# Stacked keys and queries: one contraction of 96 rows for three products of 32, and the values of the same step last in a slot

## The reference

```python
x = x + 0.5 * ffn(layernorm(x))            # weights rounded to -1, 0, 1 times a scale
x = x + attention(layernorm(x))
x = x + 0.5 * ffn(layernorm(x))

# attention: x is 4 x 1024 x 512, 16 heads of 32
kqv = x @ Wqkv + bqkv                      # q, k, v
scores = einsum('bsnh,btnh->bnst', k, q) / sqrt(32)
scores = triu(scores) - 10000 * tril(ones, k=-1)
attn = softmax(scores, axis=2)             # over the last index
out = einsum('bnkq,bknh->bqnh', attn, v)
out = out.reshape(b, s, 512) @ Wo + bo
```

## Time and profile before

| | |
|---|---|
| median of 3 runs | 1118.87 us (1113.22 to 1119.31) |
| the profiled execution | 1115.44 us, its span 1113.7 us |
| PE busy | 1067.9 us (96% of the span) |
| PE weight loads | 691.1 us (62%) |
| ACT busy | 921.7 us (83%) |
| DVE busy | 738.9 us (66%) |
| POOL busy | 344.0 us (31%) |
| granted clock of PE | 0.983 of full speed over the run |

### The profile page before, as it was taken

The page is one execution under the profiler, slowest core; times in us unless marked ns, Lnnn a source line. Parts: engine busy times, 40 slices in busy tenths (PEclk is TensorE's granted clock), DMA queues, the critical chain, the costliest instruction groups (busy, mean ns, idle before and its releaser), DMA issues.

```text
span 1113.7 us, 26124 instructions
## 1 busy us (share of the span) xinstructions
PE 1067.9 (96%) x9472; PEld 691.1 (62%) x9472; DVE 738.9 (66%) x2306; ACT 921.7 (83%) x2577; POOL 344.0 (31%) x471
## 2 busy tenths in 40 slices
PE   5799999999999999999999999999999999999896
PEld 3576656565666565665666666675666666665465
DVE  6866577787535767789644766789744667765344
ACT  2269998999989989889988988878988998999641
POOL 3841232233001313345201322435401322311343
PEclk8898999999999999999999999999999999998999
DMA  6463211021004110421112211421112212000121
GB/s 207 153 217 125 97 50 40 3 78 50 24 19 154 32 59 31 158 73 43 38 41 87 77 59 50 144 78 40 51 40 86 69 40 69 21 12 13 60 66 38
DMA packets 42015, 77.71 MB, mean 70 GB/s; under 512 B 5536, under 2 KB 11680, under 8 KB 41888
## 3 DMA queue, kind: packets, MB, share of 16 engines
q1 hardware_dynamic: 41888, 76.04, 20.5%
HBM read 49.81 MB, written 25.17 MB: 67 GB/s over the span
## 4 chain that ended last, share of the span: by engine, by line
PE 76%; ACT 11%; DVE 6%; issue 2%; POOL 2%; DMA 1%; SPq 0%; DVEq 0%; ACTq 0%; POOLq 0%
PE bank L1173 31%; PE bank L1294 10%; PE bank L1232 10%; PE bank L1266 10%; PE bank L1195 7%; ACT masked_scores L1073 6%; ACT prob L1099 4%; PE bank L1184 3%; PE bank L1274 3%; DVE masked_scores L909 2%; DVE st L859 1%; DMA xt<-in_L_attn_x_dram 1%; DVE hn L878 1%; POOL xt L769 1%; PE bank L1251 1%
## 5 line engine op out<-in xcount | busy, mean ns | idle before, releaser
L909 DVE CUSTOM_DVE_ANT_0 masked_scores<-bank,mask 128x512 f32<-128x512 f32 (+3 forms) x768 | 379.6, 554 | 221.3 <-PE bank L1232 220.2
L1073 ACT ACTIVATE masked_scores<-masked_scores,mst 128x512 f32<-128x512 f32 (+3 forms) x768 | 467.7, 620 | 2.9 <-DVE mst L909 2.9
L1099 ACT ACTIVATE prob<-bank 128x512 f32<-128x512 f32 (+1 forms) x640 | 302.0, 559 | 58.5 <-PE bank L1274 57.4
L1173 PE MATMUL bank<-hT,wqk 128*128 128x512 f32 x768 | 190.9, 397 | 0.0
L808 POOL TENSOR_SCALAR_AFFINE_SELECT prob<-prob 128x512 f32<-128x512 f32 (+1 forms) x96 | 78.6, 819 | 346.5 <-ACT prob L1099 345.8
L1266 PE MATMUL bank<-qT,kT 32*128 32x512 f32 (+2 forms) x2304 | 169.6, 378 | 4.5 <-DVE kT L886 1.6
L1232 PEld LDWEIGHTS bank<-kT,qT 32*128 32x128 f32 x2304 | 94.4, 185 | 115.6 <-issue 52.8
L1232 PE MATMUL bank<-kT,qT 32*128 32x512 f32 (+2 forms) x2304 | 161.2, 377 | 3.4 <-ACT prob L1099 2.6
L1173 PEld LDWEIGHTS bank<-hT,wqk 128*128 128x128 f32 x768 | 140.4, 188 | 37.9 <-ACT prob L1099 8.2
L1073 ACT ACTIVATION_READ_ACCUMULATOR masked_scores<-masked_scores,mst 128x1 f32 x768 | 156.4, 204 | 0.0
L1266 PEld LDWEIGHTS bank<-qT,kT 32*128 32x128 f32 x2304 | 97.7, 185 | 70.4 <-issue 48.4
(11 more groups left out here) (87 smaller groups left out, 971.7 us busy)
## 6 DMA issues: line engine op xcount, KB each, us to landing
wqk<-weight_scratch SPq DMA_DIRECT2D x30, 512.0 KB, 3.4
wvo<-weight_scratch SPq DMA_DIRECT2D x20, 512.0 KB, 6.0
xt<-in_L_attn_x_dram SPq DMA_DIRECT2D x32, 256.0 KB, 4.2
residual_scratch<-xt SPq DMA_DIRECT2D x32, 256.0 KB, 2.0
xt<-residual_scratch SPq DMA_DIRECT2D x32, 256.0 KB, 3.1
out_dram<-xt SPq DMA_DIRECT2D x32, 256.0 KB, 2.0
o<-in_L_attn_Wqkv_dram SPq DMA_DIRECT2D x12, 256.0 KB, 4.7
weight_scratch<-o SPq DMA_DIRECT2D x6, 512.0 KB, 3.0
```

The costliest lines, as they stand in the source:

```text
L909: nc.vector.tensor_tensor_reduce(masked_scores[:, h, at:at + n], psum(u, h)[:, at:at + n], mask[:, off:off + n], -SCALE, BIG, ALU.add, ALU ...
L1073: nc.scalar.activation(of, of, ACT.Exp, bias=mst[:, c + kc, to:to + 1], scale=-1.0, accum_out=ssum[:, c + kc, to:to + 1]).then_inc(a_free, 1)
L1099: nc.scalar.activation(prob[:, at % 2, h, off:CW], psum(("S", b, n), h)[:, off:CW], ACT.Exp, scale=SCALE)\
L1173: m = nc.tensor.matmul(psum(u), left(x, k), right(y, k), start=(n == 0), stop=(n == len(terms) - 1))
```

## The change

Keys and queries are kept stacked. The weights' columns are put in another order (`heads_inside`), so that a partition of a projection is 4*q + h; ACT and DVE write its high and low parts to one buffer `stage`, and three DMAs of 256 KB (`stack`) lay them out as 3 x 32 rows with the four heads behind each other: keys HI, LO, HI in `kst`, queries HI, HI, LO in `qst`. Rows 96 and 97 hold ones in `kst` and the two parts of the negated maximum in `qst`. There are three buffers of each; `MOVES` says in which slot SP issues a stack, the slot after the projection or the one in which its buffer's last scores are made.

A bank of scores is then one matmul of 98 rows for each block of keys, a bank of maxima one of 96 rows, head after head, each head with a semaphore of its own.

Other edits: `prob` has room for six heads in place of eight; `masked_scores` for two in place of four, so that DVE's maximum of head h waits for ACT's sum of head h - 2; ACT does the exponentials of heads 0 and 1, then the sum of head 3 of the block before, then heads 2 and 3; PE does the values of a slot's step last in that slot. `mrow` has one place in place of two. The projections of a group come in the order K0, Q0, Q1, K1, in slots 8 and 9 of one group and 1 and 2 of the next, and some transposes and products move by a slot.

```diff
 def pieces(b, g):
-    second = (Q_, K_) if g == 0 else (K_, Q_)
-    return [("P", b, g, K_, 0), ("P", b, g, Q_, 0)] + [("P", b, g, j, 1) for j in second]
+    return [("P", b, g, K_, 0), ("P", b, g, Q_, 0), ("P", b, g, Q_, 1), ("P", b, g, K_, 1)]
 GROUP0_ROWS = (
-    "C P | A | LO",
+    "C | A | LO",
...
-    "T3.2 F2.1 | A | X3.5",
-    "F2.2 P | A",
+    "F2.1 P | A | X3.5",
+    "T3.2 P | A",
...
+def outlived(u):
+    n = 2 * (u[1] * GROUPS + u[2]) + u[4] - NPIECE
+    if n < 0:
+        return None
+    last = (6, 9) if u[3] == K_ else (2, 9)
+    return n // 2 * STEPS + last[n % 2]
+MOVES = [[] for _ in SLOTS]
+for at, s in enumerate(SLOTS):
+    for u in s.uses():
+        if u[0] == "P":
+            old = outlived(u)
+            MOVES[at + 1 if old is None else max(at + 1, SLOT_OF[old])].append(u)
...
+            def stack(u):
+                sp.wait_ge(ring_free, freed(u))
+                if outlived(u) is not None:
+                    sp.wait_ge(s_full, 4 * outlived(u) + 4)
+                n, _ = piece(u)
+                to, parts = (kst[n], (HI, LO, HI)) if u[3] == K_ else (qst[n], (HI, HI, LO))
+                for j, part in enumerate(parts):
+                    sp.dma_start(to[HD * j:HD * j + HD, :, :].bitcast(F32), stage[:, part, :].bitcast(F32))\
+                        .then_inc((kst_in if u[3] == K_ else qst_in)[n], 16)
...
# DVE, maximum
-                    if EARLIER[u] is not None:
-                        dve.wait_ge(a_free, block_at(EARLIER[u], h))
+                    dve.wait_ge(ring_full, full(u) - 3 + h)
+                    if h >= 2:
+                        dve.wait_ge(a_free, block_at(u, h - 2))
+                    elif EARLIER[u] is not None:
+                        dve.wait_ge(a_free, block_at(EARLIER[u], h + 2))
...
# ACT, high part of a projection
+                    at = PROJECTIONS.index(u)
+                    if at:
+                        act.wait_ge(*stacked(PROJECTIONS[at - 1]))
...
# ACT, a slot
                 if s.step is not None:
-                    act.wait_ge(s_full, step(b, s.step) + 1)
-                    if step(b, s.step) >= 2:
-                        act.wait_ge(value_done, step(b, s.step) - 1)
-                    exponentials(b, s.step)
+                    exponentials(b, s.step, (0, 1))
                 if k and SLOTS[k - 1].blocks:
                     block_sums(SLOTS[k - 1].blocks[-1], (3,))
+                if s.step is not None:
+                    exponentials(b, s.step, (2, 3))
...
# PE, scores: three rounds of 32 rows and one of 2 go, in their place:
+                for h in range(4):
+                    bank_free(u, h)
+                    for kb, off, at in parts:
+                        key = P * (kb % QPC)
+                        m = nc.tensor.matmul(psum(u, h)[:, at:at + CW - off], keys_of(b, g, kb // QPC)[0:ROWS, h, key:key + P],
+                                             queries_of(b, g, c)[0:ROWS, h, off:CW], start=(kb == keys[0]), stop=(kb == keys[-1]))
+                    m.then_inc(s_full, 1)
...
# PE, a slot
                 if n is not None:
                     scores(b, n)
-                if n is not None and step(b, n):
-                    done = (b, n - 1) if n else (b - 1, NSTEP - 1)
-                    values(*done)
                 for u in s.uses():
                     use(u)
+                if n is not None:
+                    values(b, n)
```

More of the change, by code:

```diff
@@ L196 @@
 LAST_GROUP1_ROWS = (
-    "C P | A | X3.5",
-    "N M T3.2 P | A",
+    "C T3.2 | A | X3.5",
+    "N M P | A",
     "F2.2 P | A | X3.6",
@@ L387, in use @@
             if u != BIAS:
-                full += 1
+                full += 4 if u[0] == "A" else 1
                 self.full[u] = full
@@ L458, in macaron_kernel @@
         hi_done = sem("hi_done")
+        kst_in, qst_in = ([sem(f"kst_in{n}") for n in range(NPIECE)], [sem(f"qst_in{n}") for n in range(NPIECE)])
         s_full, s_exp = sem("s_full"), sem("s_exp")
@@ L549, in before, with keys_of, queries_of, stacked @@
             return (b, g - 1) if g else (b - 1, GROUPS - 1)
-        def query_piece(b, g, c):
-            return qT[:, (group(b, g) * CHUNKS + c) % 3, :, :]
+        def keys_of(b, g, kc):
+            return kst[piece(("P", b, g, K_, kc))[0]]
+        def queries_of(b, g, c):
+            return qst[piece(("P", b, g, Q_, c))[0]]
+        def stacked(u):
+            n, times = piece(u)
+            return (kst_in if u[3] == K_ else qst_in)[n], 48 * times
+        def place(n, h):
+            return (4 * n + h) % NPROB
+        def head_runs(n):
+            m = min(4, NPROB - place(n, 0))
+            return [(0, m)] + ([(m, 4 - m)] if m < 4 else [])
         def chunk(b, n):
@@ L707, in _ @@
                         store(u)
+                for u in MOVES[k]:
+                    stack(u)
                 for n in SLOTS[k - 1].weights if k else []:
@@ L1093, in high_output, with exponentials @@
                 i.then_inc(o_hi, 1)
-            def exponentials(b, n):
+            def exponentials(b, n, heads):
                 off = live(n % STEPS)
                 at = step(b, n)
-                for h in range(4):
-                    nc.scalar.activation(prob[:, at % 2, h, off:CW], psum(("S", b, n), h)[:, off:CW], ACT.Exp, scale=SCALE)\
+                for h in heads:
+                    act.wait_ge(s_full, 4 * at + h + 1)
+                    if 4 * at + h >= NPROB:
+                        act.wait_ge(value_done, (4 * at + h - NPROB) // 4 + 1)
+                    nc.scalar.activation(prob[:, place(at, h), off:CW], psum(("S", b, n), h)[:, off:CW], ACT.Exp, scale=SCALE)\
                         .then_inc(s_exp, 1)
```

204 lines of the change are left out of this document (100 added, 104 removed).

## The result

The changed kernel took 1409.6 us (median of 4 runs, 1407.0 to 1410.3) against 1116.2 us for the kernel before (1113.2 to 1119.3) beside it. The ratio is 1.262, 95% interval 1.258 to 1.267. The forecast was 1170 with a range up to 1228: the direction was right, the size was off by 240 us, and the time lies outside every case that I had weighed.

What follows compares the result with a forecast made beforehand. PE was taken to set the pace, ACT having 9% to spare; PE's 34 us saving was outweighed by gates and coupling. Group terms and 6 us for the head, +54.5 on 1115.4, gave 1170 us; range 1122 to 1228.

Steps and rivals of the forecast that it cites:

- the paragraph on the stacks: Three DMAs on SP take 4 us to land; ACT's next high part waits for them, at no cost in steady slots.
- 6 us for the head: Ahead of 100 us, in slots of 3.8 us, the stacks show: about 2 us for each of three pairs.
- The rival "much slower": Stacks land 6 us or more after the low part; ACT stands 1.5 us x 31, 47 more, 1217; chance 0.16.
- The order: Values in their own step's slot wait for exponentials and mask, starting 3.2 or 4.0 us after the scores start.
- the group that I had written out: The ten slots of the group from 339.7, priced one by one: 62.4 us against 60.2, +2.2.
- the third group of a batch: The group from 462.8, where DVE's rest makes slots 6.7 to 7.7 us long: 74 against 68.8, +5.2.
- the first and the last batch: Batch 0's groups +1.5, 2.6, 2.6 and 1.2 us; batch 3's +2.2, 4, 3 and 5.
- PE's 34 us: Full matmuls for scores and maxima leave PE less to do: the 160 slots sum to 903 us, from 937.
- The look at the larger of PE and ACT slot by slot: Over the 160 slots the larger of both sums to 975 us before any gates, against 973 before the change.
- the wait for the mask in front of the values: In diagonal steps values also wait for POOL's mask (0.68 us and its wait), starting 4.0 us after the scores start.
- DVE's wait for ACT's sums: With two places in `masked_scores`, maxima of heads 2 and 3 wait for sums at about 4.0 to 5.4 us in the slot.
- PE's busy time would fall: Sign to look for: PE's busy time falls while its idle time rises, in front of values and pieces behind the maxima.

Runs made afterwards that it cites:

- e4: The changed kernel with two `stage` buffers in turn and four heads of `prob` in place of six: 1281.0 us, ratio 1.145.
- e7: The changed kernel without its stack transfers, ACT's high part and the maxima waiting for DVE's low part instead, scores from cleared buffers: 1219.2 us, ratio 1.090.
- e10: The changed kernel without stack transfers, with four places of `masked_scores` and four heads of `prob`: 1186.7 us, ratio 1.062.
- e11: The changed kernel without stack transfers, with values of the step before behind the scores and four places of `masked_scores`: 1133.3 us, ratio 1.014.

## Why the prediction was wrong

**Where the time went.** Taken off one after the other: stacks 190 us (1409.6 to 1219.2), values last 52 (to 1167.0), two places of maxima 34 (to 1133.3), and 15 for what is left. The first three are taken in one order only; in another they come out otherwise (39 for the values with stacks in place, 37 for the places). Of the 190, at least 129 went through the one `stage`; since e4 also has only four heads of `prob`, which can only add waits, it is a lower bound. Cheaper copies get back nearly the same sum (141) by shortening the same waits, so the two sums overlap.

**The step that failed** is in the paragraph on the stacks: "three of 256 KB ... lie between 3 and 6, I take 4", and "so I cost them at nothing in the steady slots, hidden by the slot between". The first is a mis-sized term, 8.1 us where 4 was taken. The far end was too near as well: the four loads that gave 6.0 didn't have this source and destination. The second, the overlap, failed as a mechanism. The cover that I named was one slot, about 6 us, less 0.75, and so it held up to a landing of some 5 us. Past that point the wait isn't paid once, at ACT: ACT's queue, DVE's low part, the ring's bank and PE's A are in series behind it, Q0's own stack starts only then, and A of slot 1 waits for that one too. What was to be hidden is two flights of 8.1 us with 1.5 us of ACT and DVE between them. The term that I did put in, 6 us for the head, measured 23.

**The rival "much slower"** had this place and this chain, with its condition ("6 us or more after the low part"), and 1217 for its price. It charged 1.5 us for each of 31 pairs; the trace has 3.9 and 4.7 us at A, 2.2 more at slot 1, and then a projection or a product 1.7 to 2.4 us longer, at the lower clock. The chance of 0.16 rested on the size of the transfers alone.

By the figures of the Trainium skill's "SBUF — State Buffer", sections on the port swizzle and on the DMA setup cost, a stack was 5.6 us, an estimate. It spoke for the right rival. The measured 8.1 us hold 1.3 us of issues in front of the third transfer, which the estimate leaves out, and the other 6.8 are above it too; so here the page's direction holds and its figure is low. No run here separates ports from queues as the reason.

**The order** was right in kind and mis-sized by 55 us, some 3 of them the clearing. e7 is the forecast without stacks, 1164 by its own sum (1170 less 6), and it took 1219. Slot by slot the group that I had written out is good, 63.9 for 62.4, and the next 69.4 for 67.5. In the third group of a batch I had 74 and it is 81.0; with four places (e10) it is 73.6, so DVE's two places were undercharged, 34 us measured where the third groups had 2.6 + 5.2 x 2 + 3 = 16 in the sum for everything. The other large part is in the first and the last batch, for which I had only scaled: 17 and 8 us more than forecast, and 7.5 at the head.

**PE's 34 us** are not there, though the prices hold for the pieces that I can compare. Where nothing waits, S and A of 512 take 1.94 us together, 1.04 and 0.90 (starts of the pieces at 481.08, 482.12 and 483.02), for 0.96 and 0.96. But e11, with every suspected wait taken out, is 15 us slower than before, and in its eight middle groups no faster. The look at the larger of PE and ACT slot by slot (975 for 973) had said that no gain was to be had, and this is what came; that this is the whole reason was argued and not tested.

**Right** were the direction, the wait for the mask in front of the values, DVE's wait for ACT's sums as the most frequent of all, 262 times, and seven slots of ten of the group written out. **Wrong** too was that PE's busy time would fall: it fell in e11 alone, by 6 us.

## What to carry to other kernels

When a value that an engine kept for its readers in place now leaves by DMA, find who may not write until the transfer has landed, and follow that engine's queue: with one staging buffer the transfer's latency belongs to every engine behind it, and a second buffer (129 us back) was worth about as much as a copy that held the DMA engines a third as long (141 back). Making the copy smaller still (123 back) bought nothing more: what was left was not bytes. Price a hiding place by how far the landing may slip before it shows. When that point lies inside the range of what is unknown, as 5 us did in 3 to 6, give the rival a large share of the chance, and take its price down the whole chain and at the lower clock. Here TensorE, with 96% of the span before, lost twice from waits of 4 us, once for the wait and once for the slower matmuls behind it.

## What the runs showed of the hardware

- Three transfers of 256 KB from 128 partitions of SBUF into 32 took 8.1 us from the first issue to the last landing, and each cost 1.93 us of all 16 DMA engines, with what it slowed beside it; 192 KB between equal partitions cost 0.65. Why the first is 2.2 times as dear by the byte stays open; 64 KB from 32 partitions into 8 cost 0.36, 1.7 times, so the width of the destination alone doesn't order them.
- Three transfers of 192 KB or of 64 KB with no load issued near them took 5.0 us from the first issue to the last landing; with loads of 256 and 512 KB around them 6.7 and 6.6.
- The stacks slow their neighbours. `xt<-residual_scratch` went from 3.1 us to 6.7, and to 4.1 with the straight copies (3.6 with no stacks):

```profile
qst<-stage SPq DMA_DIRECT2D x96, 256.0 KB, 5.9
residual_scratch<-xt SPq DMA_DIRECT2D x32, 256.0 KB, 2.0
xt<-residual_scratch SPq DMA_DIRECT2D x32, 256.0 KB, 6.7
```

  The write to the scratch stayed at 2.0, the value from which I had taken my lower end.
- One issue on SP takes 0.5 to 0.7 us (three in 1.93), so three transfers put 1.3 us on the last of them before it starts.
- Behind 4.7 us of idle time on PE twelve full matmuls took 5.3 us in place of 2.9, at a granted clock of 0.52 in that window; behind 3.9 and then 2.2 us of it 4.6, at 0.62.
